# Cross-attention and a quantised FFN on one NeuronCore: another order of the first two attention batches on TensorE, ScalarE and VectorE

## The reference, cut to what matters

```
x: (16, 256, 512), ctx: (16, 256, 512), float32
# attention: 16 batches of 256 rows, 16 heads of 32
xn = layernorm(x)
q, k, v = xn @ Wq.T + bq, ctx @ Wk.T + bk, ctx @ Wv.T + bv      # 512 x 512 weights
q, k = rope(q), rope(k)
p = softmax(causal(q @ k.T / sqrt(32)))
x = x + (p @ v) @ Wo.T + bo
# feed-forward on layernorm(x): every stage is rounded to a 16-bit grid whose
# step comes from the largest absolute value of the whole stage
h = qdq(layernorm(x)); up = qdq(h @ Wu.T); gate = qdq(h @ Wg.T)    # 1536 wide
gate = qdq(gate * sigmoid_u16(gate)); o = qdq(gate * up)
x = x + o @ Wd.T
```

## Time and profile before

| | us |
|---|---|
| median of 3 runs | 1518.01 (1515.42 to 1520.56) |
| the profiled execution's own time | 1518.15 |
| its span in the trace | 1516.3 |
| busy in the span: TensorE | 1371.1 (90%) |
| busy: VectorE, ScalarE, GpSimd | 1185.9 (78%), 966.8 (64%), 341.8 (23%) |

### The profile page before, as it was taken

The page is one execution under the profiler, slowest core; times in us unless marked ns, Lnnn a source line. Parts: engine busy times, 40 slices in busy tenths (PEclk is TensorE's granted clock), DMA queues, the critical chain, the costliest instruction groups (busy, mean ns, idle before and its releaser), DMA issues.

```text
span 1516.3 us, 24371 instructions
## 1 busy us (share of the span) xinstructions
PE 1371.1 (90%) x9186; PEld 772.9 (51%) x9186; DVE 1185.9 (78%) x1794; ACT 966.8 (64%) x2024; POOL 341.8 (23%) x326
## 2 busy tenths in 40 slices
PE   4899999999999999969999999999999107999999
PEld 3566676666666666634444444444444003444444
DVE  6778888888888888756888987888899797566541
ACT  6788888888888887766322224998888783222210
POOL 1354454454445554420111110000000000000000
PEclk9899999999999999979999999999999657999999
DMA  6011111211121111133533334666789999666522
GB/s 245 29 57 57 63 56 65 71 70 71 71 71 57 57 43 43 36 101 130 181 111 125 130 113 148 243 247 229 249 317 325 416 412 351 229 217 221 200 97 84
DMA packets 93333, 228.94 MB, mean 151 GB/s; under 512 B 8480, under 2 KB 8608, under 8 KB 90272
## 3 DMA queue, kind: packets, MB, share of 16 engines
q1 hardware_dynamic: 92208, 220.04, 40.6%
q10 hardware_dynamic: 1008, 7.34, 1.2%
HBM read 144.51 MB, written 82.84 MB: 150 GB/s over the span
## 4 chain that ended last, share of the span: by engine, by line
PE 32%; DVE 8%; DMA 6%; ACT 6%; issue 2%; SPq 1%; POOL 0%; ACTq 0%; DVEq 0%
PE ffn_banks L1225 17%; PE ffn_banks L1210 15%; DVE qg L1514 3%; ACT qg L1322 2%; DMA ffn_ring<-gates_dram 2%; DMA ffn_wide<-ups_dram 2%; DVE ffn_peaks L1408 2%; DMA signs_dram<-qg 1%; ACT ffn_rest L1269 1%; DMA ffn_ring<-ups_dram 1%; DVE ffn_rest L1512 1%; ACT ffn_ring L1326 1%; SPq L1147 1%; DVE ffn_ring L1497 1%; DVE ffn_wide L1401 0%
## 5 line engine op out<-in xcount | busy, mean ns | idle before, releaser
L1210 PE MATMUL ffn_banks<-ffn_wide,ffn_rest 128*128 128x512 f16 x2304 | 500.0, 380 | 3.7 <-DVE ffn_wide L1396 2.7
L1210 PEld LDWEIGHTS ffn_banks<-ffn_wide,ffn_rest 128*128 128x128 f16 x2304 | 225.7, 98 | 277.8 <-issue 3.4
L1225 PE MATMUL ffn_banks<-ffn_rest,ffn_wide 128*128 128x512 f16 x1152 | 250.8, 381 | 83.0 <-DVE ffn_wide L1553 83.0
L1225 PEld LDWEIGHTS ffn_banks<-ffn_rest,ffn_wide 128*128 128x128 f16 x1152 | 113.1, 98 | 220.7 <-issue 86.2
L640 ACT ACTIVATE qg<-score_banks,neg_max 128x128 f32<-128x128 f32 (+1 forms) x512 | 208.4, 454 | 19.5 <-DVE neg_max L512 19.5
L1361 ACT ACTIVATE ffn_u_steps<-ffn_ring,ffn_scales 128x1024 int16<-128x1024 f32 x48 | 55.2, 1150 | 158.2 <-DMA ffn_ring<-ups_dram 152.7
L1269 ACT ACTIVATE ffn_rest<-ffn_banks,ffn_row_back 128x1024 f32<-128x1024 f32 x72 | 79.6, 1106 | 103.3 <-PE ffn_banks L1210 97.8
L417 POOL TENSOR_TENSOR qg<-qg,per_sum 128x512 f32<-128x512 f32 x64 | 82.6, 1291 | 268.2 <-DVE per_sum L516 268.2
L419 POOL TENSOR_TENSOR qg<-qg,per_sum 128x1024 f32<-128x1024 f32 x64 | 134.1, 2096 | 0.0
L640 ACT ACTIVATION_READ_ACCUMULATOR qg<-score_banks,neg_max 128x1 f32 x512 | 122.7, 240 | 0.0
L649 ACT ACTIVATE pt<-ring_banks 128x512 f32<-128x512 f32 x128 | 70.7, 615 | 41.9 <-PE ring_banks L776 41.0
(11 more groups left out here) (190 smaller groups left out, 2642.9 us busy)
## 6 DMA issues: line engine op xcount, KB each, us to landing
ups_dram<-ffn_rest SPq DMA_DIRECT2D x48, 512.0 KB, 3.8
ffn_ring<-ups_dram SPq DMA_DIRECT2D x48, 512.0 KB, 5.3
gates_dram<-ffn_rest SPq DMA_DIRECT2D x24, 512.0 KB, 2.6
ffn_ring<-gates_dram SPq DMA_DIRECT2D x24, 512.0 KB, 4.5
signs_dram<-qg SPq DMA_DIRECT2D x24, 512.0 KB, 4.3
ffn_wide<-ups_dram SPq DMA_DIRECT2D x12, 1024.0 KB, 17.5
qg<-signs_dram SPq DMA_DIRECT2D x24, 512.0 KB, 10.9
ffn_rest<-w_parts_dram SPq DMA_DIRECT2D x36, 256.0 KB, 4.0
```

Of the source, the lines that this page charges most:

```text
L1210: last = pe.matmul(banks[:, pair_of(s), half, :], w[:, m % 2, wp, c, :], xq[:, xp, n, c, :], start=(k == 0), stop=(k == 3 * DC - 1))
L1225: last = pe.matmul(down_banks[:, g % 2, t, :], oq[:, g % 2, op, m, t * P:(t + 1) * P], w_down[:, wp, wk, c], start=(start and k == 0), sto ...
```

## The change

Three strings get another order; no step is added or removed, and no instruction changes its shape.

- TensorE: after `S0 MX2` it did `MX1 QK2 V1 S1 XT0+1 XT1+1 QK3 V0`. Now it does `QK2 MX1 QK3 XT0+1 S1 XT1+1 V1 V0`. Group 1's scores, the projection of group 3 and the two transposes of batch 1 stand ahead of V's first products. From `QK0+1` on the order is as before, and as many ring banks have been filled.
- ScalarE: `sumw0 sumw1` stand ahead of `xn0 xn1`; `cthi0` follows `xthi0` directly; the two `xn` of batch 1 change places; between `raw2` and `raw0+1` the order is `cthi1+1 cthi0+1 raw3 xthi1+1 hi5 xthi0+1 Vev1 exps1 Vev0 xn0+2`. `sumc+3` goes from ahead of `exps2` to between the two `xthi` of batch 2.
- VectorE: `ctlo0 lo1` come first after `scale0`; `bn0+1` moves behind `rope0`, `rope1` ahead of `scale1 scale2`, both `bn` of batch 2 ahead of `lo4`, and `recip0` behind `lo4`.
- GpSimd's string and the loads stay as they are.

```diff
--- before.py
+++ after.py
@@ -121,15 +121,15 @@
-PE_BEGIN = ("MX0 XT0 XT1 QK0 QK1 S0 MX2 MX1 QK2 V1 S1 XT0+1 XT1+1 QK3 V0 QK0+1 PT0 S2 PV0 PT1 QK1+1 S3 PV1 XT0+2 "
+PE_BEGIN = ("MX0 XT0 XT1 QK0 QK1 S0 MX2 QK2 MX1 QK3 XT0+1 S1 XT1+1 V1 V0 QK0+1 PT0 S2 PV0 PT1 QK1+1 S3 PV1 XT0+2 "
             "XT1+2 MX3 PT2 QK2+1 V0+1 PV2")
-ACT_BEGIN = ("xn0 xn1 sumw0 sumw1 xthi0 hi0 cthi1 cthi0 xthi1 hi1 hi2 hi3 sumc+1 raw0 sumw2 sumw3 raw1 xn1+1 xn0+1 "
-             "exps0 hi4 raw2 Vev1 xthi0+1 xthi1+1 hi5 cthi1+1 cthi0+1 exps1 raw3 Vev0 raw0+1 pte0 xn0+2 sumc+2 "
-             "othi0 sumc+3 exps2 pte1 xn1+2 raw1+1 othi1 xthi0+2 xthi1+2 exps3 pte2 cthi0+2 xn1+3 raw2+1 othi2 "
-             "cthi1+2")
-DVE_BEGIN = ("bn0 bn1 rs dsum0 dsum1 scale0 xtlo0 lo0 ctlo1 ctlo0 xtlo1 lo1 bn1+1 lo2 lo3 bn0+1 rope0 max0 scale2 "
-             "scale1 rope1 recip0 bn0+2 lo4 max1 xtlo1+1 xtlo0+1 bn1+2 ctlo1+1 ctlo0+1 rope2 recip1 rope3 max2 "
-             "otlo0 rope0+1 lo5 recip2 max3 otlo1 xtlo0+2 xtlo1+2 scale3 bn0+3 bn1+3 recip3 rope1+1 ctlo0+2")
+ACT_BEGIN = ("sumw0 sumw1 xn0 xn1 xthi0 cthi0 hi1 hi0 cthi1 xthi1 hi2 hi3 sumc+1 raw0 sumw2 sumw3 raw1 xn0+1 xn1+1 "
+             "exps0 hi4 raw2 cthi1+1 cthi0+1 raw3 xthi1+1 hi5 xthi0+1 Vev1 exps1 Vev0 xn0+2 raw0+1 pte0 sumc+2 "
+             "othi0 exps2 pte1 raw1+1 xn1+2 othi1 xthi0+2 sumc+3 xthi1+2 exps3 pte2 cthi1+2 cthi0+2 raw2+1 othi2 "
+             "xn1+3")
+DVE_BEGIN = ("bn1 bn0 dsum0 rs dsum1 scale0 ctlo0 lo1 xtlo0 lo0 ctlo1 xtlo1 lo2 bn1+1 lo3 rope0 bn0+1 max0 rope1 "
+             "scale1 scale2 bn1+2 bn0+2 lo4 recip0 ctlo1+1 max1 xtlo1+1 ctlo0+1 xtlo0+1 rope2 recip1 rope3 max2 "
+             "otlo0 rope0+1 recip2 lo5 max3 otlo1 xtlo0+2 xtlo1+2 scale3 bn1+3 bn0+3 recip3 rope1+1 ctlo0+2")
 POOL_BEGIN = "stat+1 norm0 stat+2 norm1 norm2"
```

## The result

The changed kernel takes 1510.57 us (median of 5 runs, 1508.95 to 1512.27) where the kernel before takes 1520.49 (median of 5, 1515.42 to 1520.95). The ratio is 0.9945, 95% interval 0.9933 to 0.9957: 0.55% faster, 8.3 us of 1518; the two medians alone are 9.9 us apart. The forecast was 8.0 us, 1510.2. Two executions among the experiments, of 3736.68 and 2101.61 us, were slow ones and count in no ratio. The profiled execution took 1510.09 us, 8.06 less than the profiled one of before.

What follows compares the result with a forecast made beforehand. Attention was taken to last as long as TensorE's work plus its opening losses. Gains of 0.57 + 4.95 + 2.65 = 8.17 us, less 0.2, gave 8.0 us off 1518.15: 1510.2 us, range 1506.8 to 1514.8.

Steps and rivals of the forecast that it cites:

- Start to S0: Opening up to group 0's first scores: `ctlo0` waits for `cthi0`, so these scores start 0.61 us later, at 29.56.
- The bounds on the ramp: QK0's clock in the opening: between 1.6 us gained and 1.0 lost; taken as 0.
- lo4: VectorE's split ahead of V1: 2.35 us instead of 3.88 without `norm0` beside it; V1 starts 0.57 us earlier.
- the work in the hole: Group 1's scores, QK3 and two transposes go ahead of V1: 4.95 us leave the stretch between V1 and V0's end.
- V1's clock: First product with V's weights: with only short pauses left it runs at 2.4 GHz, gaining 2.65 us.
- the one after V1: ScalarE behind V1 and V0: `sumc+3` keeps MX3 waiting, costing between 0 and 1.17 us; taken as 0.2.
- My own sign of being wrong: Opening to batch 1: a lead of 8 us at 60 us that is gone at 110 would show the forecast wrong.
- The rival of the clock: Clock falls in the pauses between 37.15 and 41.6; V1 costs 2.65 us more, time 1512.0 to 1512.8; chance 0.24.
- Nothing: Up to group 3, ScalarE or VectorE sets the pace; 1 to 4 us are left, 1514 to 1517; chance 0.11.
- The port rival: `norm0` goes ahead of `ctlo1+1`, delaying the splits and QK0+1 by 2.7 to 3 us; time 1513.0; chance 0.08.
- x's load ahead of `lo4`: `bn1+2` ahead of `lo4` waits for x's load; at 14 us landing time the kernel takes 1522.8; chance 0.05.

Runs made afterwards that it cites:

- before again: The kernel before, unchanged, in another execution with its trace: 1518.16 us.
- V1's extra matmuls: The kernel before with 34 extra matmuls of 512 columns in TensorE's pause ahead of V1: 1516.38 us, ratio 0.9983.
- S1 alone: The kernel before with only group 1's scores moved ahead of V1 on TensorE: 1516.80 us, ratio 0.9981.
- TensorE's string alone: The changed kernel's TensorE order with ScalarE's and VectorE's orders of before: 1520.12 us, ratio 1.0022.
- again: The changed kernel, unchanged, in another execution with its trace: 1506.98 us.
- the sum: The changed kernel with `sumc+3` back ahead of `exps2`, between `sumc+2` and `othi0`: 1511.67 us, ratio 0.9952.
- the port: The changed kernel with `recip0` back ahead of batch 2's `bn` pair and `lo4`: 1512.57 us, ratio 0.9971.
- sum and `lo5`: The changed kernel with `sumc+3` ahead of `othi0` and `lo5` moved from behind `recip2` to behind `scale3`: 1512.75 us, ratio 0.9971.
- its pauses filled: The changed kernel with 24 extra matmuls ahead of QK0 and 5, 4 and 7 more in three later TensorE pauses: 1506.11 us, ratio 0.9920.

## Why the prediction was right, and where it was not

**Start to S0.** 0.61 us late was worked out. Over all executions with the same instructions up to there, S0 starts at 28.95, 29.10, 30.77, 29.98 and 30.60 in the old order (before, before again, V1's extra matmuls, S1 alone, TensorE's string alone), mean 29.88; in the new order at 30.64, 30.15, 30.79, 30.43 and 30.50 (changed, again, the sum, the port, sum and `lo5`), mean 30.50. The difference is 0.62. With 1.8 us between the earliest and the latest of the old order, an agreement to 0.01 is chance; the ten traces bear out no more than that the delay is small. In the two traces that I had first it is 1.69, since the trace of before has the shortest ramp of the five (QK0 4.25 us, 5.00 in the changed kernel). The bounds on the ramp, 1.6 gained to 1.0 lost, held this.

**lo4, the work in the hole, V1's clock.** From S0 to V1 it was 42.51 - 30.64 = 11.87 us, against 41.60 - 29.56 = 12.04 worked out. Two parts were measured by themselves: the clock 2.6 us, the port 1.4 us. Of the work moved into the hole only S1 was, and its 1.45 is in that trace; the 3.5 us of QK3 and the two transposes are seen in the changed kernel's trace and were not tried alone. The lead at V0's end was 7.25, that is 8.17 less the 1.08 of the longer ramp, within 0.2 us.

**The step that was mis-sized is the one after V1**, "between 0 and 1.17; I take 0.2". In the execution without falls the lead from group 3 to batch 3 goes from 9.15 to 8.12, about 1 us: 0.57 up to batch 1's first scores, and 0.47 behind them, where the transposes of group 3's probabilities wait 0.68 us for `norm3` (0.22 before). `sumc+3` did make MX3 wait, as I had it. But with the sum out of the way nothing was gained, as `norm2` was as late; so the term has two causes that cover each other, and I had one. And I had looked for a fall of the clock ahead of V1 alone. The falls came behind two later pauses, MX3's of 1.05 us and one of 1.72 us in batch 1 which is in the old order too, and they cost 2.3 us together. I had also worked the lock of the port for `norm0` and not for `norm2`, where `recip2` had just been moved ahead of `lo5`.

**The term that I did not have** is the end of attention. I wrote that the lead would be there as a whole at 600 us and shift the rest. It is there (5.2 or 8.2 us), and then 3.2 us more come in, where the two falls of before are absent in both traces of the changed kernel. All thirteen traces agree on what the falls cost there: from S0 of batch 15 to the first feed-forward product it is 52.8 us in the six without a fall at these two places, 54.4 in the two with one (the port, sum and `lo5`), and 55.9 to 56.1 in the five with two. So one costs 1.6 us. Nor do the falls go with the order: TensorE's string alone, 3.3 us slower than before, has none, and the changed kernel with its pauses filled has both, and no more than its 10.2 us of batch 15 at the first feed-forward product. Nothing in the forecast led to these 3.2 us, and why the falls are absent in the two traces of the changed kernel was not tried.

So the 8.0 us was met, in the first trace, as 5.18 + 3.15, and that the two add up to the forecast is luck. In the second trace the worked-out lead is there in full (8.2), and with the 3.2 behind it the gain is 11.2. The timed executions have no traces, so what their 8.3 us are made of isn't known. My own sign of being wrong, a lead of 8 us at 60 that is gone at 110, came in part in the first trace: 8.7 us at group 3 had gone down to 5.4 by 105 us. The rival of the clock had the right mechanism at the wrong pause. "Nothing" (ScalarE or VectorE as the pace, so that the lead is eaten) came true for about 1 us. The port rival did not come, as `ctlo1+1` started ahead of `norm0`. x's load ahead of `lo4` was no issue: VectorE found the tile there.

**What stays open:** what decides whether a given pause drops the clock. Pauses of 1.05 and 1.72 us did so in one execution of the same kernel and not in another, while both executions of before had their falls at the same places. So 3.2 us of the gain in the traces hang on something that this case doesn't explain. And which of ScalarE's and VectorE's moves the order of TensorE needs, apart from `raw3` and `recip0`, wasn't tried.

## What to carry to other kernels

When an engine's strict order leaves a hole, count what stands behind the hole and needs nothing of it, and then check each bank and each wait of the other engines' orders: the same move on one engine alone cost 3.3 us here, with all three 8 us were gained. A pause of TensorE costs its own length and, at times, as much again or more in the clock behind it (2.65 us behind 8.09, 1.7 behind 1.72), so price the pauses that are left, and not just the one that is taken away. Where the pause can't be closed, matmuls whose result is overwritten by the next step are worth trying: ahead of QK0 they brought 3.2 us (0.9924 against 0.9945). In three more pauses they brought nothing that the timing can tell (0.9920). And compare two kernels at several marks: a total of 8.06 us, so near the forecast, was two numbers with different causes.

## What the runs showed of the hardware that I had not expected

- Pauses of 1.05 us (ahead of MX3) and 1.72 us were followed by a granted clock of 0.51 and 0.54 in one execution, and by 1.00 in another of the same kernel, with the pauses equal to 0.01 us. This alone moved batch 3 by 2.3 us. The Trainium skill (TensorE: Matmul & The Clock Gate, The HAM clock gate) says that the moment of release varies from run to run. The traces agree (QK0 took 4.25 to 5.09 us in ten executions, by when its clock rose), and here the fall varied too.
- In the pause of 4.50 us ahead of QK0, which follows a short stretch of transposes, 24 small matmuls of a constant against a mask (4.71 us) were enough for QK0 to run at 2.4 GHz from its start, and S0 came 1.94 us earlier.
- `norm2`'s first instruction took 3.04 us beside a VectorE instruction that had started 0.16 us ahead of it, and 1.04 us when that was moved.
- A fall of the granted clock near the end of attention cost 1.6 us each time: 52.8, 54.4 and 56.0 us for the same stretch with none, one and two of them, in thirteen traces.
